# Cross attention on one core: both values pairs of a slot first, then eight transposes in one block

## What is computed

```python
q = split_heads(hidden_states @ w_q)
k, v = split_heads(text @ w_k), split_heads(text @ w_v)
out_text = sdpa(q, k, v)                       # softmax over the 56 text keys
k_ip, v_ip = split_heads(ip_h @ w_k_ip), split_heads(ip_h @ w_v_ip)
out_ip = sdpa(q, k_ip, v_ip, mask=mask_ip)     # softmax over the 8 box keys
out = (merge(out_text) + merge(out_ip)) @ w_out + b_out + hidden_states
```

## Time and profile before

| | us |
|---|---|
| median of 3 runs | 930.02 (929.28 to 930.37) |
| span of the profiled execution | 927.5 |
| TensorE busy in it | 894.0 (96%), 4685 matmuls |
| VectorE busy | 732.2 (79%) |
| ScalarE busy | 605.7 (65%) |
| GpSimd busy | 520.5 (56%) |

### The profile page before, as it was taken

How to read it: one execution, slowest core, us unless ns; L and a number is a source line. 1 busy time by engine, 2 the same in 40 slices (tenths; PEclk the granted TensorE clock), 3 DMA queues, 4 the chain that set the end, 5 groups by cost and what they waited for, 6 DMA issues and landing times.

```text
span 927.5 us, 13827 instructions
## 1 busy us (share of the span) xinstructions
PE 894.0 (96%) x4685; PEld 749.3 (81%) x4685; DVE 732.2 (79%) x999; ACT 605.7 (65%) x982; POOL 520.5 (56%) x422
## 2 busy tenths in 40 slices
PE   7999869999999999999999999999999999999978
PEld 7977748888878788888888788888888887888856
DVE  6484888888787969787887879787887879697872
ACT  5464767585848577675858586775768485866751
POOL 3372638465573929374664839283755739292731
PEclk9999999999999999999999999999999999999989
DMA  8684020303030210303030301203030302010001
GB/s 264 222 275 162 22 71 1 121 1 128 1 121 1 72 55 4 116 0 127 0 120 0 121 6 38 83 0 127 0 120 0 127 0 91 22 47 12 35 23 57
DMA packets 34151, 64.79 MB, mean 70 GB/s; under 512 B 4428, under 2 KB 6604, under 8 KB 33996
## 3 DMA queue, kind: packets, MB, share of 16 engines
q1 hardware_dynamic: 32812, 61.82, 20.2%
q10 hardware_dynamic: 1312, 2.62, 0.9%
HBM read 40.84 MB, written 23.59 MB: 69 GB/s over the span
## 4 chain that ended last, share of the span: by engine, by line
PE 58%; DVE 18%; POOL 6%; issue 5%; ACT 2%; DVEq 0%; POOLq 0%
PE bank L104 15%; PE bank L106 14%; PE bank L105 14%; PE bank L870 7%; DVE total L764 5%; DVE xT_lo L118 5%; PE bank L879 4%; PE bank L880 4%; POOL prob L551 3%; DVE res L773 3%; POOL prob L606 2%; ACT prob L651 1%; DVE o_raw L753 1%; DVE top L758 1%; DVE pT_lo L746 1%
## 5 line engine op out<-in xcount | busy, mean ns | idle before, releaser
L618 POOL TENSOR_TENSOR oT_lo<-o_raw,oT_hi 128x512 fp32r<-128x512 f32 x80 | 103.3, 1292 | 266.2 <-ACT oT_hi L671 266.2
L551 POOL TENSOR_TENSOR prob<-prob,top 128x1120 f32<-128x1120 f32 x124 | 174.4, 1435 | 0.0
L557 POOL TENSOR_TENSOR prob<-prob,inv 128x1120 f32<-128x1120 f32 x124 | 164.4, 1361 | 6.9 <-DVE inv L766 6.9
L104 PE MATMUL bank<-xT_hi,wq_hi 128*128 128x512 f32 x400 | 163.0, 408 | 2.6 <-DVE qT_lo L136 2.6
L104 PE MATMUL bank<-oT_hi,wo_hi 128*128 128x512 f32 x400 | 159.8, 400 | 3.1 <-DVE res L773 2.3
L105 PE MATMUL bank<-oT_lo,wo_hi 128*128 128x512 f32 x400 | 158.0, 395 | 0.0
L106 PE MATMUL bank<-oT_hi,wo_lo 128*128 128x512 f32 x400 | 157.9, 395 | 0.0
L106 PE MATMUL bank<-xT_hi,wq_lo 128*128 128x512 f32 x400 | 157.0, 393 | 0.0
L105 PE MATMUL bank<-xT_lo,wq_hi 128*128 128x512 f32 x400 | 155.9, 390 | 0.0
L753 DVE TENSOR_TENSOR o_raw<-bank,pv_part 64x512 f32<-64x512 f32 x160 | 110.2, 689 | 49.1 <-ACT pv_part L667 45.1
L758 DVE TENSOR_REDUCE top<-prob 128x20 f32<-128x1120 f32 (+1 forms) x128 | 98.7, 814 | 43.6 <-POOL prob L606 43.3
(11 more groups left out here) (88 smaller groups left out, 1754.3 us busy)
## 6 DMA issues: line engine op xcount, KB each, us to landing
outT<-res SPq DMA_DIRECT2D x80, 256.0 KB, 6.7
xin<-in_xT SPq DMA_DIRECT2D x14, 1280.0 KB, 6.7
w_raw<-in_L_xattn_w_v SPq DMA_DIRECT2D x8, 320.0 KB, 5.3
w_raw<-in_L_xattn_w_k SPq DMA_DIRECT2D x8, 320.0 KB, 3.6
w_raw<-in_L_xattn_w_v_ip SPq DMA_DIRECT2D x8, 320.0 KB, 3.8
w_raw<-in_L_xattn_w_k_ip SPq DMA_DIRECT2D x8, 320.0 KB, 3.7
xin<-in_xT ACTq DMA_DIRECT2D x2, 1280.0 KB, 8.0
v_raw<-v_scratch SPq DMA_DIRECT2D x16, 160.0 KB, 4.2
```

What stands on the lines that cost most here:

```text
L104: nc.tensor.matmul(dst, a_hi, b_hi, start=first, stop=False)
L551: ins = eng.tensor_tensor(s, s, top[:, t, n, :].unsqueeze(2).broadcast_to([P, HEADS, k1 - k0]), ALU.subtract)
L557: ins = eng.tensor_tensor(s, s, inv[:, t, n, :].unsqueeze(2).broadcast_to([P, HEADS, k1 - k0]), ALU.mult)
L618: nc.gpsimd.tensor_tensor(oT_lo[:, m, :], o_raw[:, m % 2, :], oT_hi[:, m, :].bitcast(F32), ALU.subtract).then_inc(oT_lo_done, 1)
```

## The change

In all three `group` functions the inner loop is split in two: first the values work of both pairs of the slot, then the transposes' work of the next two pairs. Waits, buffers and instructions are the same.

```diff
@@ ScalarE
                         for p in (2 * s, 2 * s + 1):
                             move_pv(g, p)
-                            if p + 2 < PAIRS:
-                                pT_part(g, p + 2)
+                        for p in (2 * s + 2, 2 * s + 3):
+                            if p < PAIRS:
+                                pT_part(g, p)
@@ TensorE
                         for p in (2 * s, 2 * s + 1):
                             pv_pair(g, p, b, new_batch)
-                            if p + 2 < PAIRS:
-                                p_transpose(g, p + 2, shared)
+                        for p in (2 * s + 2, 2 * s + 3):
+                            if p < PAIRS:
+                                p_transpose(g, p, shared)
```

## The result

The changed kernel takes 931.29 us (median of 12 runs, 930.14 to 932.94) against 929.94 us for the kernel before (12 runs, 928.88 to 931.63). The ratio is 1.0019, with a 95% interval from 1.0011 to 1.0026. It is slower by 1.35 us, and the forecast was +2.1 (932.1 us, range 930.9 to 934.4). The interval lies wholly above 1, so the loss is real, but it is small: 0.15% by the medians and 0.19% by the ratio, under the 0.2% (1.9 us) that the forecast named as its bound. The profiled span is 928.3 us against 927.5.

A forecast was written before the change was run, and what follows sets the result against it. TensorE was taken to bound 14 of 16 groups, a three-engine chain groups 0 and 15. Terms of 0, 0 and 2.03 us on the 930.02 us median gave 932.05, say 932.1 us, range 930.9 to 934.4.

The forecast's parts named there:

- Which groups pay: Whole kernel: the 14 middle groups lose 0.0 us, uncovered groups 0 and 15 lose 2.03 us.
- rival B: Groups 0 and 15: faster VectorE handovers, slots about 3.5 us, loss only 0.4 us, total 930.4; chance 0.10.
- Term 1: TensorE, transposes to matmuls: fewer switches save nothing, 1.34 us before against 1.33 after, priced 0.0 us.
- rival D: TensorE, middle groups: each transpose block really costs 0.08 us extra, so 4.5 us gained, total 927.5; chance 0.05.
- The prediction's sign against this term: Middle groups on TensorE: a slot shorter than 3.88 us would overthrow the claim that switches cost nothing.
- Term 2: Middle groups: query matmuls cover the pT_lo chain, 0.94 us against 0.90 needed, margin 0.04, priced 0.0 us.
- Rival A: Middle groups stall too: second pT_lo 0.71 us behind the first, 2.0 us more, total 934.1; chance 0.18.
- Term 3: Groups 0 and 15, without cover: second add delays pT_lo, slots 3.70 us, +0.99 and +1.04, in sum 2.03 us.
- Rival C: Group 15: TensorE stays longer at the lower clock, in slots and output matmuls, up to +6 us, 938; chance 0.05.

The follow-up runs named there:

- e1: Changed order in groups 0 and 15 alone, the 14 middle groups as in the kernel before: 932.37 us, ratio 1.0024 to the kernel before.
- e2: Changed order in the 14 middle groups alone, groups 0 and 15 as in the kernel before: 929.54 us, ratio 0.9997.
- e5: Changed kernel plus a small VectorE memset between adds and pT_lo in slots 0 to 3 of the middle groups: 937.08 us, 1.0081 to the kernel before.
- e11: The changed kernel measured once more, unaltered, in a later comparison: 931.39 us, ratio 1.0025 to the kernel before.
- e8: Changed kernel, but VectorE keeps its old order in groups 0 and 15: 940.14 us, ratio 1.0112 to the kernel before.
- e3: Kernel before, with ScalarE's oT_part moved behind the first pair's pT_part in groups 0 and 15: 928.79 us, ratio 0.9987.
- e7: Kernel before, with changed order in the middle groups and ScalarE's oT_part last in the slot in groups 0 and 15: 929.76 us, ratio 0.9998.
- e6: Kernel before, with ScalarE's oT_part moved behind everything in the slot in groups 0 and 15: 930.40 us, ratio 1.0010.
- e4: Kernel before, with two of each four transposes put between a pair's two matmuls in the middle groups: 933.11 us, ratio 1.0040.

## Why the prediction was right

**Which groups pay.** Right. e1 alone carries the loss, and e2 alone is no change. The number is less good than the account: +1.35 lies inside the stated range (931.29, range 930.9 to 934.4) but below the forecast's own +1.5 to +2.5. It is in the range because that took in the upper edge of rival B, whose mechanism the rows deny. The second comparison gave +1.87.

**Term 1, the switch costs nothing.** Right against rival D. The block of eight takes 0.79 to the next matmul and 0.32 to the one after (491.85, 492.64, 492.96), as in the earlier trace rows. But a block fewer is worth 0.007 us on average: e2 gains 0.32 us between groups 1 and 13, the changed kernel 0.36. The step priced this at 0.0 by 1.34 against 1.33, which is 0.01 a slot, or 0.5 us over 12 groups. That hundredth was rounded away and was the right sign. The statement that a gain is excluded in the middle, since TensorE has no idle time to win there, was wrong: a busy engine can still gain from its own order. The prediction's sign against this term, a middle slot shorter than 3.88, did come by its letter: 3.878 in the mean of 52 slots instead of 3.883. It is a fifteenth of the 0.08 that rival D asked for each slot, and it lies in the first slot of a group.

**Term 2, the cover holds by 0.04.** Right. The distance was to be 0.94 and was 0.93 to 0.95; no pair of group 7 has idle time before it. Rival A falls: it needed the second `pT_lo` 0.71 behind the first, and it is 0.60 (1.29 for two) in the new place as in the earlier trace rows. The rule named for it, the Trainium skill's (VectorE: DVE Perf Modes, "The DRAIN you can't avoid"), is not what the rows of two `pT_lo` show. But the prediction quoted half of it: that section adds that a next operation which is not held starts earlier, so these rows don't contradict it. e5 shows what such a delay costs: for 0.17 more on VectorE, 0.15 in one slot and 0.06 in another. One irregular place is left: group 14 of the changed kernel has slots of 4.02 and 4.09, 0.14 and 0.21 longer than the others, where before TensorE waited once for 0.27 ahead of pair 9. In both kernels the add of pair 4 starts 0.37 to 0.38 late there. Why it does stays open.

**Term 3, 2.03 us in the edge groups.** The mechanism and the sign were right, the size was a little high: +0.91 and +0.86, in sum 1.77. In group 0 the loop was to be 3.70 and was 3.64, 3.65, 3.72 and 3.72, with 0.60 from pair 8 to pair 9, as forecast. The step took one value, 1.12, from a pair's second matmul to its add, and that is 1.13 in the last two full slots (135.50 to 136.63) but 1.06 in the first two (128.13 to 129.19). The kernel's text has a difference at just this place: the add of an even pair waits for `oT_lo` too, but in group 0 that wait has a count of 0 up to pair 2 and is left out. In group 15, where it is always made, the second slot has 1.45 from pair to add already, against 1.37 in group 0. So the value read in group 7, which has the wait, was right for the later slots only. In group 15 pair 2 was forecast at 4.45 and came at 4.40. Pair 3 was to be 0.88 behind it at the lower clock and came 0.76 behind (894.10 to 894.86), since the full clock was back at 893.1. The second slot is 3.73 and not 3.88. Rival B falls: it needed slots of about 3.5. (The loop at which the sum crosses 1.9 is 3.68 and not 3.67, since eight slots of 0.03 less take 0.24 from 2.03.)

**What the sum left out.** Two things: +0.18 behind pair 9 of group 15, where the two last adds now stand together in front of the last output matmuls (the step said that only those and their stores stand behind, and stopped there), and -0.26 from where the lower clock began. With the middle's -0.36 they bring 1.77 down to 1.33, and the medians differ by 1.35. That the sum and the median agree so well is luck in part: the second profile of the changed kernel is 2.18 above the kernel before from the same pair on (805.01), with the lower clock in group 0's slots.

**Rival C, a longer lower clock.** It fell for the time as a whole, but its mechanism is there: e1's group 15 had it until 900.0, e11's group 0 from 126.0 to 132.7, and a slot then takes 4.40 instead of 3.65 to 3.72. The output matmuls behind group 15, the larger part of the rival's +6, stayed at the full clock in the profiles of the changed kernel and of e1; in e8 the first of them are 0.43 apart until 918 us. Single profiles don't tell whether the change makes such stretches more frequent, for e3 and e7, with the old order in the edge groups, have more of them than the kernel before too. The mean granted clock of every run tells more. The kernel before has 0.994 to 0.998 in all 73 runs of the three comparisons. Of the 36 runs with the changed order in the edge groups (changed, e1, e5, e11) 12 have less, 0.987 to 0.993, and in e8 all four. The kernels with the old order there have it in 4 of 71: two of e6 and two of e7, whose adds wait for POOL. The four such runs among 20 of the changed kernel took 932.2 to 933.6 us. So the rival's mechanism adds 1 to 2 us in about one run of five, and the medians hardly show it.

## What to carry to other kernels

Regrouping work costs next to nothing where the engine that would wait has other work to cover the chain, so price it at the first and last rounds of the loop, where there is no cover, and follow it to the last instruction that the moved ones release. Compare the margin of the cover with the handovers before moving more into it: here it was 0.04 us, and 0.17 more on VectorE cost 3.7 us. A per-round gain of a hundredth of a microsecond is read from stretches of many rounds, not from two rows, and place by place: here one slot of four had nearly all of it.

## What was not expected of the hardware

- The matmul behind a block of transposes is shown 0.47 or 0.48 us long after two, four or eight of them (0.39 or 0.40 elsewhere), while two blocks more lengthen a slot by 0.02 us: the difference of 0.08 is no time of the engine.
- A VectorE write of 0.11 us takes 0.17 us in its queue (add to `pT_lo` 1.61 instead of 1.44).
- TensorE can lose time without an idle stretch in the view: in e4 and e5 no bracket stands at the pairs of group 7, and the loss shows only in the distance to the second matmul (0.34 or 0.31 instead of 0.23) and in the slot.
- The length of the setup up to pair 0 of group 0 differs by 3 us between executions (123.99 to 127.01), more than the change under study.
- In the edge groups the granted clock goes to 0.50 at different places in different executions: 126.0 to 132.7 in one profile of the changed kernel and not at all in the slots of group 0 in the other.
